# Sixteen instead of eight indirect DMAs between waits, map scatters begun one pass earlier, softmax totals moved into the slot passes, and a rewritten relation layer, in a four-module graph network

## What is computed

```python
x = _layernorm(x + _L0_gnn_ref(x, edge_index, edge_attr_128, ...))   # 4 layers of graph attention
x = _layernorm(x + _L1_gnn_ref(x, src, dst, edge_type_5, ...))       # 3 relation layers
x = _layernorm(x + _L2_gnn_ref(x, ...))                              # 3 SAGE layers
x = _layernorm(x + _L3_gnn_ref(x, node_vec1, edge_attr_4, ...))      # one tensor-product layer

# _L0: one attention layer
h = x @ W
alpha = leaky_relu((h @ a_s)[src] + (h @ a_d)[dst] + (ea @ We) @ a_e, 0.2)
alpha = _segment_softmax(alpha, dst, N)
out = segment_sum(h[src] * alpha[:, None], dst) + b    # then a layer norm; every node is its own neighbour too
# _L1: one relation layer
msg = relu(h_in[src] + relv[rel])
red = segment_sum(msg, dst) / max(count, 1)            # the mean over a node's edges
new_h = red @ W.T + b                                  # h = h_prev + new_h from the second layer on
```

## Time and profile before

| | |
|---|---|
| time, median of 3 runs | 5679.07 us (5675.7 to 5679.91) |
| profiled execution, its own time | 5695.59 us |
| its span | 5693.8 us |
| granted TensorE clock, mean | 0.811 |
| PE busy | 3896.0 us (68%) |
| DVE busy | 3796.9 us (67%) |
| ACT busy | 3325.9 us (58%) |
| POOL busy | 2876.8 us (51%) |

### The profile page before, as it was taken

How to read it: one execution, slowest core, us unless ns; L and a number is a source line. 1 busy time by engine, 2 the same in 40 slices (tenths; PEclk the granted TensorE clock), 3 DMA queues, 4 the chain that set the end, 5 groups by cost and what they waited for, 6 DMA issues and landing times. The chain is left out here.

```text
span 5693.8 us, 104950 instructions
## 1 busy us (share of the span) xinstructions
PE 3896.0 (68%) x23663; PEld 3200.5 (56%) x23663; DVE 3796.9 (67%) x10843; ACT 3325.9 (58%) x11867; POOL 2876.8 (51%) x2759
## 2 busy tenths in 40 slices
PE   5462889556846673668277687867768787986775
PEld 5451778445525552645266454546657676775665
DVE  2671889568837883878266566767758676665665
ACT  2120889457837783878254354547768687564554
POOL 0356765502550355045400576766546574767776
PEclk8896999778977897889655676777779999997777
DMA  8993999545844684568344344645559798764221
GB/s 174 210 303 108 373 366 273 160 124 169 278 150 140 184 271 152 140 200 275 121 123 117 126 145 149 187 157 172 167 192 303 252 308 282 221 216 76 61 65 56
DMA packets 918273, 1074.23 MB, mean 189 GB/s; under 512 B 202779, under 2 KB 565065, under 8 KB 917106
## 3 DMA queue, kind: packets, MB, share of 16 engines
q1 hardware_dynamic: 763570, 890.24, 48.1%
q0 software_dynamic: 90944, 180.06, 12.9%
q10 hardware_dynamic: 63556, 1.81, 1.5%
HBM read 509.54 MB, written 566.14 MB: 189 GB/s over the span
## 5 line engine op out<-in xcount | busy, mean ns | idle before, releaser
L2319 POOL DMA_INDIRECT H<-gat_rows,src_i x784 | 801.2, 1022 | 1186.2 <-POOLq L79 633.5
L1864 POOL DMA_INDIRECT s_G<-sage_rows,src_i x588 | 601.2, 1022 | 375.7 <-issue 161.9
L1653 POOL DMA_INDIRECT r_G<-rel_rows,idx x392 | 442.4, 1129 | 221.6 <-issue 129.3
L2508 PE MATMUL p_M<-Wg,p_hT 128*128 128x132 f32 x2352 | 339.2, 288 | 61.1 <-DVE p_res L2565 46.4
L1664 PE MATMUL r_t<-r_oh,relv 8*128 8x512 f32 x294 | 229.8, 870 | 191.0 <-DMA r_G<-rel_rows,idx 68.1
L2508 PEld LDWEIGHTS p_M<-Wg,p_hT 128*128 128x128 f32 x2352 | 293.1, 193 | 110.3 <-issue 94.3
L2565 DVE SCALAR_TENSOR_TENSOR p_res<-p_M,p_rr,cg 128x132 f32<-128x132 f32 x1176 | 334.4, 348 | 2.6 <-PE p_M L2508 1.6
L1565 DVE TENSOR_TENSOR_SCAN r_agT<-same_run,r_agT,r_mT 128x512 f32<-128x512 f32 (+1 forms) x144 | 184.7, 1282 | 226.2 <-ACT r_mT L1698 224.5
L1322 PE MATMUL d_S<-ones,d_sqT 128*128 128x1 f32 x1568 | 245.0, 277 | 123.6 <-DVE d_ve L1409 123.6
L1322 PEld LDWEIGHTS d_S<-ones,d_sqT 128*128 128x128 f32 x1568 | 237.0, 231 | 156.7 <-issue 125.6
L2647 PEld LDWEIGHTS p_pl_p<-Wn,p_pl_h 128*128 128x128 f32 x1568 | 202.9, 196 | 203.8 <-ACT p_pl_h L2741 156.9
(11 more groups left out here) (469 smaller groups left out, 12540.7 us busy)
## 6 DMA issues: line engine op xcount, KB each, us to landing
gat_rows<-p_res SPq DMA_DIRECT2D x294, 264.0 KB
sage_rows<-p_pl_s SPq DMA_DIRECT2D x294, 256.0 KB
gat_rows<-x_row SPq DMA_DIRECT2D x98, 536.0 KB, 5.5
gat_rows<-d_res SPq DMA_DIRECT2D x147, 264.0 KB
d_hs<-gat_rows SPq DMA_DIRECT2D x147, 256.0 KB
s_hT<-sage_slots_t SPq DMA_DIRECT2D x147, 256.0 KB
slot_rows<-H SPq DMA_DIRECT2D x49, 544.0 KB, 11.5
x_x<-in_x SPq DMA_DIRECT2D x98, 256.0 KB
```

Of the source, the lines that this page charges most:

```text
L1653: pool.indirect_dma_start(self.G[:, g % 4, k, :], None, table, bass.IndirectOffsetOnAxis(index[:, c:c + 1], 0), bounds_check=bound, oob_is ...
L1864: pool.indirect_dma_start(self.G[:, g % 4, k, :], None, kn.st[self.l], bass.IndirectOffsetOnAxis(kn.idx[:, c:c + 1], 0), bounds_check=boun ...
L2319: pool.indirect_dma_start(kn.H[:, c, 0:width], None, table, bass.IndirectOffsetOnAxis(index[:, c:c + 1], 0), bounds_check=bound, oob_is_er ...
L2508: mm = pe.matmul(self.pM[self.bank(b, j)][:, k // 2, (k % 2) * TW:(k % 2 + 1) * TW], self.hT[l][:, b.s2, k * P:(k + 1) * P], kn.Wg[:, l, : ...
```

## The change

1. `RING` is 16: the wait for the whole batch comes before every sixteenth scatter or gather, 12 times in 196 instead of 24.
2. The first 24 map scatters (`EARLY`) are issued in the graph's pass, the other 172 in the x pass; the index tile is computed in the graph's pass.
3. The totals are no longer in `soft(l)` but are "once" steps, (step, lag, 1), at the head of the lists of DVE and PE in `slots(l)`. `times()` no longer lets such short steps shorten the loop. The spare tiles `lt`, `res` and `n0` hold the intermediates.
4. In d3 the list of ACT begins with `deviation2`.
5. `RelSlots`: the gathered rows are multiplied with `share_squares` instead of the identity, and the one-hot kinds with the same share, so that the relu's result is already divided by the count. `means` is gone, `mix` reads the product from PSUM. `bias` becomes `next_bias`, in r0 and r1, whose result `yb` is what is stored for the next layer. `spread_shares` moves from s0 to r0. In r2 the tiles `oh`, `agT` and `y` have two buffers instead of four (Y = 2), `nrm` and `res` too, and SP's two stores have lags 11 and 12 instead of 13 and 14.

```diff
-RING = 8
+RING = 16
@@ def times
-    lo, hi = max(lag for _, lag, _ in steps), min(lag + k for _, lag, k in steps)
-    lo = max(lo + 4, PEEL)
+    lo = max(max(lag for _, lag, _ in steps) + 4, PEEL)
+    hi = min(lag + k for _, lag, k in steps if lag + k > lo)
@@ def graph
+            @block.gpsimd
+            def _(pool):
+                pool.wait_ge(mr, 1)
+                pool.wait_ge(self.self_mapped, 16 * (self.G + 1))
+                self.place_in_map(pool, 0, self.EARLY)
...
+                v.tensor_scalar(self.mput[:, :], pf[1][:, K:2 * K], float(2 * T0W // 4), float((GB + MAP) // 4), ALU.mult, ALU.add).then_inc(mr, 1)
...
-                    last = v.tensor_scalar(kind[:, n, :, :], mine[:, :, :, R_TYPE], float(n), None, ALU.is_equal)
+                    last = v.scalar_tensor_tensor(kind[:, n, :, :], mine[:, :, :, R_TYPE], float(n), fill[:, 1], ALU.is_equal, ALU.mult)
...
+    EARLY = 24
+
+    def place_in_map(self, pool, first, end):
+        for c in range(first, end):
+            if c and c % RING == 0:
+                for j in range(RING):
+                    pool.wait_ge(self.placed[j], c // RING * 16)
...
@@ def dense0
-                for c in range(K):
...
+                self.place_in_map(pool, self.EARLY, K)
@@ def slots
+                once = [(turn_weights, 0, 1), (turn_ends, 1, 1), (turn_carries, 2, 1), (turn_totals, 3, 1)]
+                times(pe, once + [(sum_squares, 5), (turn, 2), (rows if end else product, 5)], KG)
...
-                times(act, core + ([(deviation2, 9), (square2, 8)] if end else [(scaled, 6), (heads, 7)]), KG)
+                times(act, [(deviation2, 9)] + core + [(square2, 8)] if end else core + [(scaled, 6), (heads, 7)], KG)
...
+                once = [(weights_of_both, 0, 1), (sums_in_rows, 1, 1), (carries, 2, 1), (carried, 3, 1), (totals, 4, 1)]
...
+                    times(v, once + [(scale2, 9), (norm, 9), (add_x, 7), (run_sums, 3), (scale, 6), (weigh, 1), (variance, 5)], KG)
@@ class RelSlots
+        self.Y = 2 if self.last else 4
...
-        return ([(load, 0)] + ([(load_prev, 2)] if l else []) + ([(load_x, 5), (store_nT, 13), (store_rows, 14)] if self.last else
+        return ([(load, 0)] + ([(load_prev, 2)] if l else []) + ([(load_x, 5), (store_nT, 11), (store_rows, 12)] if self.last else
...
+                share = kn.shares[:, bass.ds(b.n * KT + k, 1), :].rearrange("p o n -> p (o n)")
+                mm = pe.matmul(pt[:, k * P:(k + 1) * P], self.G[:, b.s4, k, :], share, start=False, stop=(k == KT - 1))
...
         def product(b):
             done(pe, self.scn, b)
-            done(pe, self.scd, b, 2)
+            done(pe, self.ym, b, 2)
...
-        def means(b):
...
-        def bias(b):
...
+        def spread_shares(b):
+            c = bass.ds(b.n * KT, KT)
+            v.tensor_tensor(kn.shares[:, c, :], spread(kn.ident[:, :], KT), fan(kn.shareD[:, c], P), ALU.mult).then_inc(self.shd, 1)
...
         def mix(b):
-            done(v, self.scd, b)
+            done(v, self.wm, b)
+            done(v, self.sq, b, self.Y)
...
+                v.tensor_tensor(self.y[:, b.m % self.Y].rearrange("p k d -> p (k d)"), self.pw[b.s2][:, :], before, ALU.add).then_inc(self.ym, 1)
...
+        def next_bias(b):
+            done(v, self.ym, b)
+            landed(v, self.ystored, b, 4)
+            v.tensor_tensor(self.yb[:, b.s4], self.y[:, b.m % self.Y], spread(kn.br[:, l + 1, :], KT), ALU.add).then_inc(self.yn, 1)
...
-                    (e["gamma"](v), 5), (bias, 3), (e["stats"](v), 6)]
-        return [(cut, 6), (mix, 4), (run_sums, 2)] + ([(bias, 3)] if l else []) + [(scale, 5), (norm, 5)]
+                    (e["gamma"](v), 5), (e["stats"](v), 6)]
+        return ([] if l else [(spread_shares, 0)]) + [(cut, 6), (mix, 4), (run_sums, 2), (next_bias, 4), (scale, 5), (norm, 5)]
```

More of the change, by code:

```diff
@@ L1337, in rows, with turn_weights, turn_ends, turn_carries @@
                     mm.then_inc(yr, 1)
-                times(pe, [(sum_squares, 5), (turn, 2), (rows if end else product, 5)], KG)
+                def turn_weights(b):
+                    pe.wait_ge(tc, 1)
+                    for g in range(2):
+                        mm = pe.transpose(psa[:, g * P:(g + 1) * P], cand[:, g * HALF:(g + 1) * HALF], ident[:, :])
+                    mm.then_inc(tt, 1)
+                def turn_ends(b):
+                    pe.wait_ge(tc, 4)
+                    for g in range(2):
+                        mm = pe.matmul(psb[:, g * HALF:(g + 1) * HALF], ends[:, g:g + 1], ident[0:HALF, 0:HALF], start=True, stop=True)
+                    mm.then_inc(tt, 1)
+                def turn_carries(b):
+                    pe.wait_ge(tc, 7)
+                    for g in range(2):
+                        mm = pe.matmul(psc[:, g:g + 1], crow[:, g * HALF:(g + 1) * HALF], self.one_row[0:1, 0:1], start=True, stop=True)
+                    mm.then_inc(tt, 1)
+                def turn_totals(b):
+                    pe.wait_ge(tc, 9)
+                    for g in range(2):
+                        mm = pe.transpose(psd[:, g * HALF:(g + 1) * HALF], F[:, g, :], ident[0:HALF, 0:HALF])
+                    mm.then_inc(tt, 1)
+                once = [(turn_weights, 0, 1), (turn_ends, 1, 1), (turn_carries, 2, 1), (turn_totals, 3, 1)]
+                times(pe, once + [(sum_squares, 5), (turn, 2), (rows if end else product, 5)], KG)
             @block.scalar
@@ L1439, in _ @@
                 if end:
-                    times(v, [(scale2, 9), (norm, 9), (add_x, 7), (run_sums, 3), (scale, 6), (weigh, 1), (variance, 5)], KG)
+                    times(v, once + [(scale2, 9), (norm, 9), (add_x, 7), (run_sums, 3), (scale, 6), (weigh, 1), (variance, 5)], KG)
                 else:
-                    times(v, [(out, 7), (run_sums, 3), (scale, 6), (weigh, 1), (variance, 5)], KG)
+                    times(v, once + [(out, 7), (run_sums, 3), (scale, 6), (weigh, 1), (variance, 5)], KG)
     def plain_tiles(self):
@@ L1698, in relu @@
             act.activation(self.mT[:, b.s2, :], self.pt[b.s2][:, :], ACT.Relu).then_inc(self.mtk, 1)
-        def means(b):
-            done(act, self.wm, b)
-            done(act, self.sq, b, 4)
-            if self.last:
-                done(act, self.gr, b, 4)
-            else:
-                landed(act, self.ystored, b, 4)
-                done(act, self.un, b, 4)
-            for k in range(KT):
-                last = act.activation(self.y[:, b.s4, k, :], self.pw[b.s2][:, k * P:(k + 1) * P], ACT.Copy, scale=kn.shareD[:, bass.ds(b.n * KT + k, 1)])
-            last.then_inc(self.scd, 1)
         def square(b):
@@ L1725, in norm @@
         def norm(b):
-            done(act, self.ntr, b, 4)
+            done(act, self.ntr, b, 2)
             self.e["norm"](act)(b)
@@ L1737, in keep_rows @@
             done(act, self.rm, b)
-            landed(act, self.rstored, b, 4)
-            act.activation(self.res[:, b.s4].rearrange("p k d -> p (k d)"), self.pr[:, :], ACT.Copy).then_inc(self.rk, 1)
+            if not isinstance(b.n, int) or b.n >= 2:
+                act.wait_ge(self.rstored[(b.m + 2) % 4], (b.i + (b.m - 2) // 4 + 1) * 16)
+            act.activation(self.res[:, b.s2].rearrange("p k d -> p (k d)"), self.pr[:, :], ACT.Copy).then_inc(self.rk, 1)
         if self.last:
-            return [(deviation, 5), (means, 3), (self.e["deviation2"](act), 7), (keep_turned, 9), (square, 4), (keep_rows, 10), (norm, 8), (relu, 1)]
-        return [(deviation, 5), (means, 3), (square, 4), (relu, 1)]
+            return [(deviation, 5), (self.e["deviation2"](act), 7), (keep_turned, 9), (square, 4), (keep_rows, 10), (norm, 8), (relu, 1)]
+        return [(deviation, 5), (square, 4), (relu, 1)]
     def vector(self, v):
@@ L1872, in turn @@
             done(pe, self.scn, b, 2)
-            if l == 0:
-                done(pe, self.shd, b)
             for k in range(KT):
```

167 lines of the change are left out of this document (79 added, 88 removed).

## The result

The changed kernel takes 5393.22 us (5388.61 to 5400.67, 4 runs) against 5679.49 us (4 runs) of the kernel before on the same chip: a ratio of 0.9492, with a 95% interval of 0.9472 to 0.9513, 286 us less. The forecast was 5350 with a range of 5300 to 5445. The profiled execution took 5400.67 us; 295 us shorter by the span.

A forecast was written before the change was run, and what follows sets the result against it. POOL's DMA chain was taken to bound x and the plain passes' tails, a loop of waits d3. Terms summed to −328 from the profiled 5695.6, giving 5367.6; 16.5 off for the median gave 5350 us, range 5300 to 5445.

The forecast's parts named there:

- rival of a batch end that costs twice: Plain passes and x: a batch of sixteen waits twice as long as one of eight; 5537 us, half 5443; chance 0.08.
- x, −51: Graph and x: early scatters and fewer batch ends let p0 start at 490 to 491 instead of 542.9; −51 us.
- Gathers, −146: Four plain passes: twelve of 24 batch ends go in each, −36 us per pass, −146 in all.
- Totals, −19: Softmax and slot passes: the totals' chain leaves softmax, −8.1, and costs slots 3.3, four times: −19 us.
- d3, −78: d3: ACT's earlier `deviation2` opens a loop of waits, leaving 234 us of 312: −78, bounds −60 to −95.
- What is late next is PE with 227.49/49 = 4.64 us per block, at a clock of 0.52: d3: once the wait goes, PE at its lower clock level bounds the pass, ahead of DVE with 4.26 us.
- if PE is granted more clock and DVE bounds: d3: the term's larger bound, −95 us instead of −78.
- r0, +8: r0: new DVE steps mostly hidden under POOL; +8 us for the first share and some collisions, +44 if cover fails.
- hidden with 0.4 to spare: r0: DVE goes from 3.8 to 5.1 us per block, staying under POOL's 5.5.
- The rule against the change: r0: two-SBUF-input DVE steps contend with POOL's gathers, +4 to +33 us; read strictly, the sum is −295.
- r2, −38: r2: a block takes 6.5 to 7.3 us instead of 7.9, 49 × −0.8 = −38 us, range −15 to −60.
- SP and landing (2.0 + 3.4): r2: SP's part and the store's landing, in us, within a store loop of 13 to 14.5 per two blocks.

The follow-up runs named there:

- both pairs: Profiles of the changed kernel and the kernel before, unaltered: the first results' (5393.22 against 5679.49 us) and later ones on another chip (5363.63, 5679.57 us).
- e9: Changed kernel, unaltered, on another chip of the first results' kind, against the kernel before: 5363.63 us, ratio 0.945.
- e12: Changed kernel without early scatters, plain-pass batches of 32, r0 shares as DVE's last step, SP's r2 stores first at unchanged lags; against kernel before: 6636.22 us, 1.0796.
- e8: Changed kernel with SP's two r2 stores ahead of its loads, lags 10 and 11, against the kernel before on a slower chip: 6484.17 us, ratio 1.043.
- e11: Changed kernel with rolling wait, r0 shares spread by ACT, SP's r2 stores first (lags 10, 11), against the kernel before, slower chip: 6656.34 us, 1.0837.
- e2: Changed kernel with no early scatters (EARLY = 0), against the kernel before on a slower chip: 6534.14 us, ratio 1.0486.
- e1: Changed kernel with batches of eight again (RING = 8), against the kernel before on a slower chip: 6111.88 us, ratio 0.9801.
- e7: Changed kernel with a rolling wait, only for DMA number c - 16, against the kernel before on a slower chip: 6726.55 us, ratio 1.0803.

## Why the prediction was right, and where it was off

**The bound and the sign.** The POOL tails behind x and the plain passes were the place, and d3's loop of waits. 286 us are gone of 329 forecast for the median, and 295 of 328 in the profile. Taken together the terms missed by more than their sum: r2 gained 24 less than forecast, r0 lost 16 more and the gathers gained 11 less, but d3 gained 19 more; that these partly cancel is luck. The rival of a batch end that costs twice is refuted on this kind of chip: 197.9 us instead of 342.1.

**x, −51.** It came to −48 and −55. The x pass started at 213 instead of 207 (the preparation took 3 us more in this execution, and the self-map, issued at 137.7, let the first scatter go at 177.0, after 39 us instead of 36), products and scatters ended together at 480 to 483.

**Gathers, −146.** It came to −135 in both pairs, 32 to 36 per pass. The mechanism was right and the size a little high. Of the 39 us per pass the term took a tenth off, 4, for slower gathers. They stayed as they were (1.022 us in the mean before, 1.026 now); what takes 7 us instead is that the 12 batch ends left are 0.56 us dearer each (197.9/48 against 342.1/96).

**Totals, −19.** −15 and −13 for the first three against −14: right, and in the way that was said: between the barriers each softmax pass is 8.1 us shorter and the slot passes d0 to d2 2 to 4 longer.

**d3, −78.** It came to −97 (101.8 less the 4.8 of its softmax part), just beyond the term's bound of −95. The step that failed is "What is late next is PE with 227.49/49 = 4.64 us per block, at a clock of 0.52". The 4.64 us were themselves the price of the low clock: with the wait gone TensorE was granted 0.74, and PE needs 166.81/49 = 3.40 us per block. One step of PE, d_Y, in the trace before, which took 1.13 us in the changed kernel:

```profile
3007.14 2.07 PE L1336 MATMUL d_Y<-Gc,d_yT 128*128 128x128 f32 x8 [1.41 <-DVE d_vv L1426]
```

What is late next is DVE, 207.44 of 215 us, 4.23 per block, which is also what a block of the steady part takes (6.52 before). The term's own bound, "if PE is granted more clock and DVE bounds", had named this case. The timeline of the changed kernel shows it: no DVE step waits, and ACT's second deviation (L1389) is done 0.6 us before DVE's reciprocal (L1472):

```profile
2746.46 0.30 ACT L1389 ACTIVATE d_sd<-d_ss,eps_c 128x4 f32<-128x4 f32 x1
...
2747.30 0.15 DVE L1449 TENSOR_TENSOR d_ve<-d_S,te 128x4 f32<-128x4 f32 x1
...
2747.38 0.17 DVE L1472 RECIPROCAL d_r<-d_sd 128x4 f32<-128x4 f32 x1
2747.57 0.20 ACT L1364 ACTIVATE d_sd<-d_ve 128x4 f32<-128x4 f32 x1 [0.81 <-DVE d_ve L1449]
...
2749.55 1.13 PE L1318 MATMUL d_Y<-Gc,d_yT 128*128 128x128 f32 x8 [0.43 <-DVE d_vv L1466]
```

**r0, +8.** It came to +24 and +30. The step that failed is "hidden with 0.4 to spare". DVE was hidden indeed, but POOL, which paces the pass, wasn't left alone: 196 gathers took 1.201 us instead of 1.097, 20.4 us more. The rule against the change had been priced at +4 to +33 and was given no weight in the sum; the first pair puts it at 20, the second at 26 (1.210 us instead of 1.077). (With its +33 the sum would have been −295, which is the span's difference to the digit; since the other terms missed too, that is chance.) In e9, one block of r0: the gather at 3004.42 starts within `cut` (L1823) and takes 1.43 us, that at 3006.15 starts beside nothing and takes 1.00, that at 3007.45 starts within the scan and takes 1.28:

```profile
3003.69 0.68 DVE L1790 TENSOR_TENSOR share_squares<-ident,shareD 128x512 f32 x1
3004.29 0.68 DVE L1823 TENSOR_TENSOR r_u<-r_u,nbb 128x512 f32<-128x512 f32 x1
3004.42 1.43 POOL L1695 DMA_INDIRECT r_G<-n_rows,src_i  x1 [0.30 <-issue]
3004.89 0.68 DVE L1802 TENSOR_TENSOR r_y<-r_w,br 128x512 f32<-128x512 f32 x1
3006.15 1.00 POOL L1695 DMA_INDIRECT r_G<-n_rows,src_i  x1 [0.30 <-PE r_t L1711]
3006.65 1.28 DVE L1605 TENSOR_TENSOR_SCAN r_agT<-same_run,r_agT,r_mT 128x512 f32<-128x512 f32 x1 [1.07 <-ACT r_mT L1743]
3007.45 1.28 POOL L1695 DMA_INDIRECT r_G<-n_rows,src_i  x1 [0.31 <-issue]
```

**r2, −38.** It came to −14, −28 and, on the slower chips, −17 to −25. In the steady part a block takes 7.5 and 7.3 us instead of 7.8, 0.3 to 0.5 less instead of 0.8. The step that failed is "SP and landing (2.0 + 3.4)": the store of the same buffer is indeed what ACT waits for, but SP's part of it is five times as long. Store and copy matched by their number, a tile's store is issued 11.3 us after the tile is ready in the kernel before (mean of blocks 9 to 40), and 10.4 in the changed one. The two lags less gave only 0.9, since the load of `r_oh` ahead of the store now waits, with two buffers instead of four, for the messages of two blocks back; with the same lags and the stores first (e12) it is 6.9. In the changed kernel:

```profile
3700.86 0.60 ACT L1767 ACTIVATE r_nT<-r_nt 128x512 f32<-128x512 f32 x1 [1.71 <-DMA sage_slots_t<-r_nT]
3701.83 2.08 PE L1711 MATMUL r_t<-share_squares,r_G 128*128 x8
...
3704.08 0.32 SPq L1652 DMA_DIRECT2D r_oh<-kinds  x1
...
3705.85 0.36 SPq L1673 DMA_DIRECT2D sage_slots_t<-r_nT  x1
...
3708.94 0.60 ACT L1767 ACTIVATE r_nT<-r_nt 128x512 f32<-128x512 f32 x1 [3.44 <-DMA sage_slots_t<-r_nT]
...
3711.43 0.36 SPq L1673 DMA_DIRECT2D sage_slots_t<-r_nT  x1
...
3715.18 0.60 ACT L1767 ACTIVATE r_nT<-r_nt 128x512 f32<-128x512 f32 x1 [1.60 <-DMA sage_slots_t<-r_nT]
```

The tile that is ready at 3701.46 is stored at 3711.43, and its buffer is written again at 3715.18, when the store has landed. The store at 3705.85 is that of the block before; it stands behind PE's messages, the load that waited for them, and two more loads. Copy, SP and landing, 0.6 + 10.0 + 3.7, make the 14.3 us of these two blocks. The prediction's own sum, 13 to 14.5, comes near with a far smaller part of SP and with norm, turn and the way to the next norm, which are not in this wait; that was luck. With the stores first SP's part is 1.1 us (e8, blocks 9 to 40) and the wait for the store is gone in e8, e11 and e12; r2 took 12 to 48 us less there.

**The rest.** The forecast took 16.5 us off for the difference between the profiled execution and the median; the changed kernel's profiled execution lies only 7.5 above its median. That is 9 of the 43 us between 5350 and 5393.

## What to carry to other kernels

An engine's busy time that was measured at TensorE's low clock isn't a bound for what comes when the waits go: price it at both levels. When a step is given to DVE beside GpSimd's DMAs, look at whether GpSimd paces the pass and at the number of the step's SBUF inputs, not at DVE's spare time: a gather that starts in such a step is held for what is left of it. A PSUM operand avoids it; so does ACT, but in r0 it delayed the messages by as much as it saved. And a queue that carries loads and stores should have the stores whose buffers are short ahead of loads that wait for something younger.

## What the runs showed of the hardware that was not expected

On three of the chips a finished step reached another engine late while POOL issued indirect DMAs, and the later the longer POOL had issued without standing still. In e2, x pass, PE's turn of one block ended at 226.0 us, and ACT had done with the copy of the block before at 237.7, but started this block's copy at 251.2; the wait is put down to no event that the trace has:

```profile
224.90 1.12 PE L1009 MATMUL x_T<-ident,x_x 128*128 128x128 f32 x4
...
237.10 0.60 ACT L1026 ACTIVATE x_xT<-x_T 128x512 f32<-128x512 f32 x1 [14.36 <-remote]
...
251.24 0.60 ACT L1026 ACTIVATE x_xT<-x_T 128x512 f32<-128x512 f32 x1 [13.54 <-remote]
```

For every copy, take the time from the moment when its turn, the product that frees its buffer and ACT's copy before were all done: in e2 it is 14.0 us in the median from 200 to 340 us (8 copies, 25.5 at most), and 0.08 once the scatters are done (80 copies, 0.12 at most); with batches of eight (e1, 79 copies up to 500 us) 0.12, with 4.5 at most; in the changed kernel of the first result 0.04, with 0.12 at most (98 copies). The windows of two batches of p1 in e2, each cut in halves, show the engines running in the first half and standing nearly still in the second:

```profile
1835.50:1847.00 11.50, 9.19 (x44) 6.20 (x43) 7.45 (x25) 6.56 (x16) 8.93 (x9) 0.87 0.70 195
1847.00:1858.50 11.50, 3.78 (x10) 2.21 (x10) 2.72 (x11) 1.46 (x4) 7.25 (x7) 0.70 0.37 104
1905.50:1917.00 11.50, 7.84 (x34) 5.37 (x34) 5.15 (x17) 6.21 (x14) 9.06 (x9) 0.80 0.50 139
1917.00:1928.50 11.50, 0.00 (x0) 0.00 (x0) 1.59 (x6) 0.00 (x0) 7.16 (x8) 0.65 0.35 93
```

These two are no exception. Over all twelve batches of p1 in e2, each cut in eighths, DVE is busy for 0.73, 0.90, 0.76, 0.57, 0.30, 0.34, 0.23 and 0.13 of the time; in e9 it is 0.79 to 0.90 in every eighth.

DVE's work of p1 that gets done while POOL gathers falls with the size of the batch. The windows are those of e1 (eight), e2 (sixteen), e12 (32), e7 (rolling) and, of the other kind of chip, e9 (sixteen):

```profile
1566.00:1897.00 331.00, 228.61 (x1088) 158.87 (x1089) 216.48 (x718) 209.65 (x477) 203.42 (x196) 0.84 0.71 213
```

```profile
1764.00:2052.00 288.00, 124.78 (x502) 83.60 (x503) 119.29 (x401) 104.85 (x241) 199.19 (x196) 0.70 0.53 147
```

```profile
1768.00:2038.00 270.00, 44.84 (x142) 28.52 (x141) 48.55 (x165) 35.14 (x81) 197.49 (x196) 0.54 0.33 87
```

```profile
1777.00:2034.00 257.00, 38.22 (x118) 24.62 (x118) 44.80 (x155) 28.80 (x66) 197.13 (x196) 0.54 0.34 84
```

```profile
1270.00:1572.00 302.00, 203.84 (x1099) 145.46 (x1098) 215.37 (x719) 210.28 (x480) 200.73 (x196) 0.87 0.79 239
```

216, 119, 49 and 45 us of DVE work with 24, 12, 6 and no batch ends: 8 to 10 us per batch for the first three (the 216 are all the work there is in the pass). There the waits at the batch ends, which the change halves, let the other engines go on, and all versions with sixteen or more were 4 to 8% slower than the kernel before, the one with eight 2% faster. On the other kind of chip all 215 us of work are done beside sixteen. What differs between the chips, and what exactly holds the events back, stays open: the length of the DMA packets doesn't differ (those of 1072 bytes in the x pass take 0.05 us on either kind), nor do the softmax and slot passes, which have none of GpSimd's DMAs. A kernel that has to run on the slower kind would keep batches of eight with the other parts of the change (e1: 0.98 there); what it takes on the first kind wasn't measured.
